# Four nodes in sequence per partition: a new node order inside the 512-node quads of a GNN kernel

## The reference

```python
def gin(x, edge_index, edge_attr):                   # W_edge, b_edge, W1, b1, W2, b2, eps, gamma, beta
    src, dst = edge_index
    msg = relu(x[src] + edge_attr @ W_edge + b_edge)
    h = (1 + eps) * x + segment_sum(msg, dst)
    h = relu(h @ W1 + b1) @ W2 + b2
    h = (h - mean(h, 0)) * rsqrt(var(h, 0) + 1e-5) * gamma + beta
    return relu(h)

def gcn(h):                                          # three layers, self loops added, norm = dinv[src]*dinv[dst]
    for W, b in ((W1, b1), (W2, b2), (W3, b3)):
        h = relu(segment_sum((h @ W.T)[src] * norm[:, None], dst) + b)
    return h

x = layernorm(x + gin(x, edge_index, edge_attr_128))
x = layernorm(x + gcn(x))
```

## Time and profile before

| | |
|---|---|
| median of 3 runs (lowest to highest) | 3551.61 us (3547.77 to 3553.03) |
| the profiled execution: its own time, its span | 3548.29 us, 3546.5 us |
| constants, search and gin_pass, to the first `zt` | 1143.8 us |
| norm_pass, first `zt` to last x1 | 1143.8 to 1582.6 us |
| first gcn_pass, second gcn_pass, last_pass | about 648, 625 and 689 us |
| PE, PEld, DVE, ACT, POOL busy | 89%, 87%, 79%, 80%, 63% of the span |
| mean DMA rate over the span | 242 GB/s |

### The profile page before, as it was taken

The page is one execution under the profiler, slowest core; times in us unless marked ns, Lnnn a source line. Parts: engine busy times, 40 slices in busy tenths (PEclk is TensorE's granted clock), DMA queues, the critical chain, the costliest instruction groups (busy, mean ns, idle before and its releaser), DMA issues. The chain is left out here.

```text
span 3546.5 us, 88756 instructions
## 1 busy us (share of the span) xinstructions
PE 3160.6 (89%) x24644; PEld 3068.2 (87%) x24644; DVE 2803.8 (79%) x7960; ACT 2846.1 (80%) x5909; POOL 2233.1 (63%) x2320
## 2 busy tenths in 40 slices
PE   3999999999996544448999999899999979999998
PEld 2999999999996444438999999799999979999998
DVE  5999999999996878766666666566666659999997
ACT  1777777777775888867888888688888859999999
POOL 3655555555550766647777775677777657766662
PEclk7999999999998555559999999999999989999999
DMA  3666656666663899987777776687777769999996
GB/s 94 192 182 183 183 175 181 184 175 176 181 186 129 311 352 361 362 287 234 256 255 252 256 252 212 211 261 255 253 256 255 237 218 322 318 318 317 315 316 227
DMA packets 655163, 859.17 MB, mean 242 GB/s; under 512 B 131005, under 2 KB 516821, under 8 KB 655056
## 3 DMA queue, kind: packets, MB, share of 16 engines
q1 hardware_dynamic: 564778, 652.15, 56.3%
q0 software_dynamic: 87024, 205.39, 18.4%
q10 hardware_dynamic: 3254, 0.43, 0.1%
HBM read 632.57 MB, written 257.52 MB: 251 GB/s over the span
## 5 line engine op out<-in xcount | busy, mean ns | idle before, releaser
L560 POOL DMA_INDIRECT rows<-x_in,node_i x490 | 592.7, 1210 | 441.3 <-DVE raw L1133 285.6
L560 POOL DMA_INDIRECT rows<-gb_scratch,node_i x441 | 450.1, 1021 | 223.3 <-issue 112.6
L560 POOL DMA_INDIRECT rows<-ga_scratch,node_i x441 | 449.2, 1019 | 184.6 <-issue 119.2
L560 POOL DMA_INDIRECT rows<-x_scratch,node_i x441 | 449.2, 1019 | 179.4 <-issue 116.8
L1526 DVE TENSOR_TENSOR gcn_agg_lo<-gcn_agg_ps,gcn_agg_hi 128x1024 fp32r<-128x1024 f32 x196 | 240.1, 1225 | 374.8 <-ACT gcn_agg_hi L1568 374.8
L588 PE MATMUL gcn_agg_ps<-gcn_select,gcn_rows_hi 128*128 128x256 f32 (+2 forms) x1960 | 501.8, 290 | 19.4 <-DVE gcn_rows_lo L1536 19.4
L588 PE MATMUL gcn_agg_ps<-gcn_select,gcn_rows_lo 128*128 128x256 f32 (+2 forms) x1960 | 483.0, 287 | 0.0
L602 PE MATMUL gcn_h_ps<-g_hi,gcn_agg_hi 128*128 128x256 f32 x1568 | 450.6, 287 | 0.0
L602 PE MATMUL gcn_h_ps<-g_lo,gcn_agg_hi 128*128 128x256 f32 x1568 | 447.8, 286 | 0.0
L602 PE MATMUL gcn_h_ps<-g_hi,gcn_agg_lo 128*128 128x256 f32 x1568 | 445.3, 284 | 0.0
L1553 ACT ACTIVATE gcn_h<-gcn_h_ps,one_by_degree 128x256 f32<-128x256 f32 x784 | 307.9, 476 | 156.8 <-PE gcn_h_ps L602 156.8
(11 more groups left out here) (202 smaller groups left out, 11225.5 us busy)
## 6 DMA issues: line engine op xcount, KB each, us to landing
own<-x_t_in SPq DMA_DIRECT2D x196, 256.0 KB, 2.6
h_scratch<-h2t SPq DMA_DIRECT2D x196, 256.0 KB, 2.9
x_scratch<-x SPq DMA_DIRECT2D x98, 512.0 KB, 5.3
gcn_own<-x_scratch SPq DMA_DIRECT2D x98, 512.0 KB, 4.4
ga_scratch<-gcn_h SPq DMA_DIRECT2D x98, 512.0 KB
gcn_own<-ga_scratch SPq DMA_DIRECT2D x98, 512.0 KB, 4.6
gb_scratch<-gcn_h SPq DMA_DIRECT2D x98, 512.0 KB, 5.1
fin_own<-gb_scratch SPq DMA_DIRECT2D x98, 512.0 KB, 5.8
```

The costliest lines, as they stand in the source:

```text
L560: pool.indirect_dma_start(out=c["rows"][:, slot, row_block(slot, b) if shared else b], out_offset=None, in_=source[:, :], in_offset=bass.I ...
```

## The change

Node 4p+j of a quad now lies on partition p in tile j. A partition's four nodes follow each other in DRAM: one run of 4 KB. Wherever the order of nodes inside a quad matters, it follows:

- `quad_rows` gives the new pattern to the x1 store and load, to the own-row loads and to the stores of `ga` and `gb`.
- In `sum_columns` the span of nodes [first, end) is now columns first/4 to end/4 of each of the four tiles: the matmul writes its columns in four runs, 128 columns apart. `select` is laid out in the same order by comparing with a new constant table, `iota_by_tile`, which holds 4n+j at [j][n].
- In `norm_pass`, ACT writes `zt` in the new column order: it reads four neighbouring elements and writes them 128 elements (512 B) apart.
- The tile of an edge is now its place modulo 4, its position in the tile the place divided by 4 (`low_i`, `high_i`).
- `x_q` and `out` are laid out to match outside the kernel.

`gin_pass` is unchanged, and so are the gathers.

```diff
@@ constants, vector
+                nc.vector.tensor_copy(c["iota_by_tile"][:].rearrange("p j n -> p n j"),
+                                      iota_i[:].rearrange("p (n j) -> p n j", j=4))
@@ quad_rows
-    return dram[bass.ds(q * QUAD, QUAD), :].rearrange("(j p) d -> p j d", p=P)
+    return dram[bass.ds(q * QUAD, QUAD), :].rearrange("(p j) d -> p j d", p=P)
@@ select_columns
-        last = nc.vector.tensor_scalar(select[:, b, 0:end - first], c["iota32"][:, first:end],
+        last = nc.vector.tensor_scalar(select[:, b, 0:end - first].rearrange("p (j n) -> p j n", j=4),
+                                       c["iota_by_tile"][:, :, first // 4:end // 4],
                                        c["place"][:, bass.ds(quad.q, 1), b], None, ALU.is_equal)
@@ sum_columns
-                last = nc.tensor.matmul(out[:, h, first:end], rows[:, quad.split_block(k), h * P:(h + 1) * P],
-                                        select[:, b, k, 0:end - first], start=False,
+                last = nc.tensor.matmul(out[:, h].rearrange("p (j n) -> p j n", j=4)[:, :, first // 4:end // 4],
+                                        rows[:, quad.split_block(k), h * P:(h + 1) * P],
+                                        select[:, b, k, 0:end - first].rearrange("p (j n) -> p j n", j=4), start=False,
                                         stop=k == BLOCKS - 1 and rows is rows_lo, skip_group_check=True)
@@ norm_pass, scalar
-                            last = nc.scalar.activation(zt[:, b, h].rearrange("p (o n) -> p o n", o=2),
-                                                        ahead.h2[quad.wide_slot][:, h:4:2],
+                            last = nc.scalar.activation(zt[:, b, h].rearrange("p (j o n) -> p o n j", j=4, o=2),
+                                                        ahead.h2[quad.wide_slot][:, h:4:2].rearrange("p o (n j) -> p o n j", j=4),
@@ norm_pass, vector
-                nc.vector.tensor_scalar(low_i[:], place_i[:], P - 1, None, ALU.bitwise_and).then_inc(split_done, 1)
+                nc.vector.tensor_scalar(low_i[:], place_i[:], 3, None, ALU.bitwise_and).then_inc(split_done, 1)
...
-                nc.vector.tensor_scalar(tile_i[:], place_i[:], 7, None, ALU.arith_shift_right).then_inc(split_done, 1)
+                nc.vector.tensor_scalar(high_i[:], place_i[:], 2, None, ALU.arith_shift_right).then_inc(split_done, 1)
...
-                nc.vector.tensor_copy(node_in_tile[:], low_i[:]).then_inc(split_done, 1)
-                nc.vector.tensor_copy(tile_of[:], tile_i[:]).then_inc(split_done, 1)
+                nc.vector.tensor_copy(node_in_tile[:], high_i[:]).then_inc(split_done, 1)
+                nc.vector.tensor_copy(tile_of[:], low_i[:]).then_inc(split_done, 1)
@@ kernel
-        "x_q": padded(x, NPAD).reshape(NQ, 4, P, D).transpose(0, 2, 1, 3),
+        "x_q": padded(x, NPAD).reshape(NQ, P, 4, D),
```

More of the change, by code:

```diff
@@ L802, in _ @@
                                 .then_inc(hist_steps, 1)
-                            nc.vector.tensor_scalar(tile_i[:], ids[:, 1:2], 7, 3, ALU.arith_shift_right, ALU.bitwise_and)\
+                            nc.vector.tensor_scalar(tile_i[:], ids[:, 1:2], 3, None, ALU.bitwise_and)\
                                 .then_inc(hist_steps, 1)
@@ L807, in _ @@
                             dve.wait_ge(hist_steps, e * 11 + 3)
-                            nc.vector.tensor_scalar(lo_i[:], node_i[:], P - 1, None, ALU.bitwise_and)\
+                            nc.vector.tensor_scalar(lo_i[:], node_i[:], 2, None, ALU.arith_shift_right)\
                                 .then_inc(hist_steps, 1)
@@ L1223, in norm_pass @@
         place_i = m.sb("place_i", [P, NQ, BLOCKS], I32)
-        tile_i = m.sb("tile_i", [P, NQ, BLOCKS], I32)
+        high_i = m.sb("high_i", [P, NQ, BLOCKS], I32)
         low_i = m.sb("low_i", [P, NQ, BLOCKS], I32)
@@ L1794, in gnn @@
             "iota16": m.sb("iota16", [P, NT], F16), "iota32": m.sb("iota32", [P, QUAD]),
+            "iota_by_tile": m.sb("iota_by_tile", [P, 4, P]),
             "rows": m.sb("rows", [P, QUAD_RING, BLOCKS, D]),
@@ L1866 @@
     result = run_bass_kernel_spmd(nc, [{name + "_in": a for name, a in arrays.items()}], core_ids=[0])
-    return result.results[0]["out"].reshape(NQ, P, 4, D).transpose(0, 2, 1, 3).reshape(NPAD, D)[:N]
+    return result.results[0]["out"].reshape(NPAD, D)[:N]
```

## The result

The changed kernel takes **3587.47 us** (median of 4 runs, 3587.19 to 3589.46) against 3551.52 us for the kernel before in the same comparison: a ratio of **1.0105** (95% interval 1.009 to 1.012), 36 us slower. 3525 us was forecast, with a range of 3512 to 3592. The time lies inside the range and on the side of rival A.

The account below looks back on a forecast made before the run. PE was taken to bound gcn_pass and last_pass, transfers norm_pass with ACT second. The x1 store's -27 us and 0 for all else gave 3521.3 us for the profiled execution, 3525 us for the median; range 3512 to 3592.

Parts of the forecast that it names:

- rival A: norm_pass: ACT's two zt instructions cost up to 0.84 us a quad, so ACT takes over; +11 to +54 us, chance 27%.
- Part 2: norm_pass: ACT's two zt instructions writing 512 B apart cost 0, with 0.84 us a quad kept for the range.
- Part 1: norm_pass: x1 store in 4 KB instead of 1 KB pieces takes a quad from 4.36 to 4.08 us, -27 us.
- The rates per share (315, 361, 390): GB/s per full DMA share: 315 for 1 KB pieces, 361 for norm_pass's mix, 390 derived for 4 KB pieces.
- the formula: Mixing 315 and 390 GB/s by bytes gave 337 for last_pass, matching the 337 measured there.
- rows 10 and 11: PE weight loads: 98 columns 32 B apart take 270 ns, 128 side by side 337; cited against a zt write cost.
- Parts 3 to 6: PE's four-run sum matmuls, DVE's select, the other 4 KB transfers, the added cast and place tables: 0 each.
- rival B: The 5880 sum matmuls writing four runs cost PE time: 3584 us at 10 ns a matmul; chance 8%.
- Rival C: norm_pass gains nothing, as memory limits it or waits between ACT, PE and DVE grow: 3552 us, chance 9%.

Follow-up runs that it names:

- first run: The changed kernel, but ACT writes zt contiguously and PE's z transposes take columns 16 B apart: 3558.73 us, ratio 1.0015.
- sixth run: The kernel before with 1 KB pieces, SP storing x1 of a quad one step later: 3534.47 us, ratio 0.9951.
- twelfth run: The kernel before with 18 copies of 512 fp32 elements ahead of it, on ACT and DVE at various steps; each copy timed once, no kernel time given.
- ninth run: As experiment 5, with ACT's square root of the degrees taken before the x1 instructions and DVE's degree sum ahead of shift: 3491.76 us, ratio 0.9832.
- experiment 5: The first run with SP storing x1 of a quad one step later: 3536.9 us, ratio 0.9958. Its 8.96 us rows show the kernel before.
- 10: The sixth run with the square root taken before the x1 instructions and the degree sum ahead of shift: 3495.96 us, ratio 0.9847.
- eleventh: The first run with x1 rows 32 B apart in SBUF, so the store goes in 1 KB packets to the same places: 3548.03 us, ratio 0.9995.
- third run: The kernel before with 1 KB pieces and only zt written 512 B apart: 3583.39 us, ratio 1.0089.

## Why the prediction was wrong

**Part 2 failed, and with it the sign.** I put the `zt` writes at 0 and left the full price to rival A. They cost 0.9% or 32 of the 36 us by which the kernel is slower (the changed kernel against the first run). The price was 798 to 1242 ns in duration, +0.44 us, a little over the bound of 0.42 for one instruction. What it costs in pace is less: in the changed kernel's timeline of ACT

```profile
1301.96 2.27 ACT L1302 ACTIVATE zt<-rows,bn_c,bn_a 128x512 f32<-128x512 f32 x2
...
1304.20 2.06 ACT L1318 ACTIVATE x<-res,ln_shift,ln_factor 128x256 f32<-128x256 f32 x4
1306.17 2.28 ACT L1302 ACTIVATE zt<-rows,bn_c,bn_a 128x512 f32<-128x512 f32 x2
```

one undisturbed quad takes 1306.17 - 1301.96 = 4.21 us, where it takes 3.56 in the sixth run, with the old write: +0.65, not +0.84. Over the stage only 0.41 is left, because part of the added work fills waits that ACT had before (27.9 us for loads, now 8.9). The choice of 0 leaned on the nearest row, a weight load of PE with columns 32 B apart. That row was right about PE (first run) and said nothing about ACT. The Trainium skill (Advanced Engine Details and Errata, SBUF Cachelines) had the rule: 16-byte lines, and at least two hits on each to hide the access. The twelfth run agrees with it in kind: two elements on a line, at 8 B, are nearly free (0.55 against 0.52 us); one, at 16 B, costs 0.87. By that rule a step of 12 B lies between: if the first element begins a line, two of every four elements share one and two stand alone, and the copy takes 0.71 us, halfway. I had put the rule below a row of another engine.

**Part 1 failed as well.** "The transfers set the pace" was read from a DMA share of 0.99 and a rate that fitted the interval. The share is no measure of a limit: the same queue carried 413 GB/s in the ninth run. The rates per share (315, 361, 390) were not properties of the pieces; with 4 KB pieces only, norm_pass showed 356 and gcn_pass 75.76 MB in 50.5% of 450 us, 333. That the formula fitted a third stretch was an accident. What held the stage was a loop in time: end of x1, wait on SP, store, issue of the next loads, landing (8.96 us for two steps in the rows of experiment 5). Around it lay the wait for the root every four quads. Both can be taken away without touching a byte (runs 5, 6, 9, 10). By itself the 4 KB store was worth not -27 but about +7 us (first run against the eleventh; against the kernel before it is 0.15%, 5 us).

**Rival A was right** in place and direction. It gave +11 to +54 us with its middle at 3584, and the time is 3587.5. The interval grew by 0.41 us a quad, and the write alone, in the third run, by 0.38: from 4.36 to (1601.2 - 1.24 - 1140.4) / 97 = 4.74. Its mechanism holds too: 4.21 us undisturbed, 42.8 / 98 = 0.44 for the shift and 8.9 / 98 = 0.09 for loads make 4.74 of the 4.77 us seen. That its middle came so near is in part luck: its price of 0.84 us was 0.19 too high, and the middle counted only half of the shift waits, 0.22, where all of them stayed. Its argument against itself, rows 10 and 11, was the weak one.

**Parts 3 to 6 were right in the sum.** Four runs of columns cost PE nothing, so rival B falls. `select` stays at 343 ns. The stages under PE keep their length, though in gcn_pass q1's share fell to 50.5% only, not to 43%. The added cast takes 0.66 us, 0.25 more than the contiguous one, and lies ahead of a wait.

**Rival C** got the worth of the store about right. It named two reasons. The first, the memory limit of 358 GB/s that I set against the trace, is not what bound the stage. The second, that waits between the engines grow into the room, is nearer to what the runs show, but it named no wait. The Trainium skill (DMA: Bandwidth & Descriptors, Where 436 GB/s comes from) names that limit as binding for transfers between HBM and SBUF; another page of the Trainium skill (HBM Reference, Specifications (TRN2)) calls the same figure the share of a core when both of a pair work, and says that one alone gets more. The ninth run, one core at work at 413 GB/s, agrees with the second.

## What to carry to other kernels

Let PE take the stepped side of a change of layout (its weight loads took it for free here, in a stage where PE was not the bound) and keep ACT and DVE at steps of two fp32 elements or less. A DMA share near 1 and a rate that fits the interval don't prove that transfers are the bound: look at what their issue waits for, and shift that wait by a step before making the transfers cheaper. And print the interval of a pipelined stage quad by quad: a pattern of four tells of a wait that a mean hides.

## What the runs showed of the hardware

- ACT, copies of 512 fp32 elements: 0.52 us from start to start at 4 B, 0.55 at 8 B, 0.71 at 12 B, 0.87 at 16 B, 0.88 at 512 B, written. Read, the durations are alike, and the starts are 0.53 us apart at 8 B, 0.78 at 12 B and 0.99 at 16 B. DVE, durations written at the same steps: 0.43, 0.42, 0.50, 0.60 and 0.69 us.
- PE, fp32 weight loads with columns 16 B apart, at a granted clock of 0.50: no cost (226 ns at the median against 230 with contiguous columns; 3558.7 us against 3559.2).
- PE, a matmul writing four runs of 64 or 80 columns 512 B apart in PSUM keeps its pace, 0.12 and 0.15 us.
- q1 with two loads and one store of 512 KB a quad carried 413 GB/s. A busy share of 0.99 was seen at 358 GB/s and of 1.02 at 413.
- 4 KB instead of 1 KB packets in one of three transfers: about 7 us slower in a stage held by the wait for x1 (the packets' size and x1's addresses in SBUF changed together). With that wait a step later and the root earlier, 4 us faster between medians, not beyond the noise.
